# A two-layer conditioned transformer on one core: first scale and first projections by feature chunks, loads in that order

## The reference

```python
def ada_rms(x, t, w, tw):
    n = x * rsqrt(mean(square(x), -1) + 1e-6)
    scale = t @ tw.T
    return n * (w * (1.0 + scale))[:, None, :]

h = ada_rms(x, time_emb, ln1_w, ln1_tw)
q, k, v = h @ Wq.T, h @ Wk.T, h @ Wv.T          # 8 query heads, 1 key/value head of 64
q, k = rope(q, pos), rope(k, pos)
x = x + softmax(q k^T / 8) v @ Wo.T
h = ada_rms(x, time_emb, ln2_w, ln2_tw)
x = x + (silu(h @ Wg.T) * (h @ Wu.T)) @ Wd.T    # inner width 2048
# then the second layer: layer norm with scale and shift from the condition (W_ada), attention with rope, add
```

## Time and profile before

| | us |
|---|---|
| median of 3 runs (lowest to highest) | 836.48 (835.95 to 837.05) |
| profiled execution | 836.44 |
| its span, first to last instruction | 834.6 |
| TensorE busy in the span | 827.2 |
| VectorE, ScalarE, GpSimd busy | 598.5, 414.1, 392.4 |

### The profile page before, as it was taken

The page is one execution under the profiler, slowest core; times in us unless marked ns, Lnnn a source line. Parts: engine busy times, 40 slices in busy tenths (PEclk is TensorE's granted clock), DMA queues, the critical chain, the costliest instruction groups (busy, mean ns, idle before and its releaser), DMA issues.

```text
span 834.6 us, 15041 instructions
## 1 busy us (share of the span) xinstructions
PE 827.2 (99%) x5688; PEld 678.6 (81%) x5688; DVE 598.5 (72%) x889; ACT 414.1 (50%) x725; POOL 392.4 (47%) x310
## 2 busy tenths in 40 slices
PE   9999999999999999999999999999999999999998
PEld 5888878888788788787888887888878878878886
DVE  6986567666665766766656878877867668678997
ACT  4555445435345344345446475373453543735662
POOL 2667535545544446446545755454443533532110
PEclk9999999999999999999999999999999999999999
DMA  9913442433523523424444445355254353330001
GB/s 334 387 34 110 137 158 98 162 119 116 175 101 104 183 92 131 158 68 154 145 154 143 144 166 196 115 177 169 83 184 155 105 196 124 124 132 14 15 27 52
DMA packets 73335, 113.50 MB, mean 136 GB/s; under 512 B 6320, under 2 KB 39088, under 8 KB 73264
## 3 DMA queue, kind: packets, MB, share of 16 engines
q1 hardware_dynamic: 72544, 112.45, 39.8%
q10 hardware_dynamic: 720, 0.09, 0.1%
HBM read 88.15 MB, written 24.38 MB: 135 GB/s over the span
## 4 chain that ended last, share of the span: by engine, by line
PE 95%; DVE 2%; DMA 1%; issue 1%; ACT 0%; POOL 0%; SPq 0%; ACTq 0%; DVEq 0%; POOLq 0%
PE ps L736 29%; PE ps L738 28%; PE ps L737 28%; PE ps L1024 2%; PE ps L834 1%; PE ps L1052 1%; PE ps L783 1%; DMA pT<-turned_p 1%; PE ps L864 1%; PE ps L775 1%; DVE ex L1529 1%; PE ps L1032 1%; PE ps L745 1%; PE ps L992 0%; DMA turned_p<-tp 0%
## 5 line engine op out<-in xcount | busy, mean ns | idle before, releaser
L736 PE MATMUL ps<-h2h,guh 128*128 128x512 f32 x512 | 203.5, 397 | 0.0
L738 PE MATMUL ps<-h2l,guh 128*128 128x512 f32 x512 | 199.9, 391 | 0.0
L737 PE MATMUL ps<-h2h,gul 128*128 128x512 f32 x512 | 199.3, 389 | 0.0
L590 POOL TENSOR_TENSOR gul<-rgu,guh 128x1024 fp32r<-128x1024 f32 x64 | 161.0, 2516 | 71.2 <-ACT guh L1890 71.2
L595 POOL TENSOR_TENSOR wdl<-rwd,wdh 128x512 fp32r<-128x512 f32 x64 | 83.5, 1304 | 129.4 <-ACT wdh L1898 129.4
L1415 DVE TENSOR_TENSOR xres<-ps,xres 128x512 f32<-128x512 f32 x128 | 87.4, 684 | 62.7 <-PE ps L738 62.7
L736 PEld LDWEIGHTS ps<-h2h,guh 128*128 128x128 f32 x512 | 96.0, 188 | 27.4 <-issue 7.7
L738 PEld LDWEIGHTS ps<-h2l,guh 128*128 128x128 f32 x512 | 96.1, 188 | 21.2
L737 PEld LDWEIGHTS ps<-h2h,gul 128*128 128x128 f32 x512 | 96.2, 188 | 19.1
L736 PE MATMUL ps<-wdh,ah 128*128 128x512 f32 x256 | 100.1, 391 | 0.0
L737 PE MATMUL ps<-wdh,al 128*128 128x512 f32 x256 | 99.6, 389 | 0.0
(11 more groups left out here) (199 smaller groups left out, 1588.1 us busy)
## 6 DMA issues: line engine op xcount, KB each, us to landing
rgu<-gu SPq DMA_DIRECT2D x64, 512.0 KB, 4.7
rwd<-WdT SPq DMA_DIRECT2D x64, 256.0 KB, 4.2
turned_q<-tq SPq DMA_DIRECT2D x20, 320.0 KB, 3.0
qkT<-turned_q SPq DMA_DIRECT2D x20, 320.0 KB, 3.2
turned_p<-tp SPq DMA_DIRECT2D x9, 512.0 KB, 2.6
pT<-turned_p SPq DMA_DIRECT2D x9, 512.0 KB, 4.0
xt<-xT SPq DMA_DIRECT2D x15, 256.0 KB, 2.9
out<-xres SPq DMA_DIRECT2D x15, 256.0 KB, 3.5
```

Source lines behind the costliest of these rows:

```text
L590: pool.tensor_tensor(gul[i][:, :], rgu[i][:, :], guh[i][:, :], ALU.subtract).then_inc(m_gul, 1)
L736: pe.matmul(dst, lh, rh, start=start, stop=False)
L737: pe.matmul(dst, ll, rh, start=False, stop=False)
L738: return pe.matmul(dst, lh, rl, start=False, stop=stop)
```

## The change

The first scale is no longer computed for all 512 features at once. `first_scale(g)` computes 128 of them, g = 0 to 3, with four products that add up in one strip of 32 columns (strip g); ScalarE copies those 32 rows, `first_scale_T(g)` transposes them to 128x32, VectorE makes the scale of chunk g of them, and chunk g of the turned `x` is scaled by VectorE for tile 0 (`scale_part`, one 128x128 multiply) and by ScalarE for tile 1 (two activations of 128x64). `first_qkv(t, k)` is now two products, of one chunk, and the chunks of both tiles alternate with the scale groups. Half of `condition_second` moves ahead of `qk_T(0)`. `ln1_tw` is laid out by output group; SyncE loads group, `WqkvT` chunk, group, chunk and so on, with `xT` of tiles 0 and 1 after the first group and chunk. The five small loads on ScalarE's queue become two, one for the positions and one (`consts`) that holds the identity, the norm weights and the rope frequencies. The loads of `ln2_tw`, `adaT` and `x` of tiles 3 to 5 are cut into parts with semaphores of their own. `square(2)`, `mean_sq(2)`, `low_h(2)`, `split_qkv` and `scale_h(2)` take other places in the lists of their engines. The last `keep_warm(3)` stays; the three single ones become one. The results are the same sums.

The core of the diff (semaphore counts and declarations left out):

```diff
@@ SyncE @@
-            sp.dma_start(condt[:, :, :], by_row(condT)).then_inc(ld_cond, 16)
-            for k in range(KT):
-                sp.dma_start(adaw0[:, k, :], by_row(ln1_twT)[:, k, :]).then_inc(ld_ln1[k], 16)
-            load_xT(0)
-            for k in range(KT):
-                sp.dma_start(wst[:, k, :], by_row(WqkvT)[:, k, :]).then_inc(ld_qkv[k], 16)
-            sp.dma_start(xres[:, 0, :], xv[:, 0, :]).then_inc(ld_x0, 16)
-            load_xT(1)
+            sp.dma_start(condt[:, :, :], condT).then_inc(ld_cond, 16)
+            for g in range(KT):
+                sp.dma_start(adaw0[:, g, :], ln1_tw[g, :, :]).then_inc(ld_ln1[g], 16)
+                if g == 0:
+                    load_xT(0)
+                if g == KT - 1:
+                    sp.dma_start(xres[:, 0, :], xv[:, 0, :]).then_inc(ld_x0, 16)
+                sp.dma_start(wst[:, g, :], by_row(WqkvT)[:, g, :]).then_inc(ld_qkv[g], 16)
+                if g == 0:
+                    load_xT(1)
             sp.dma_start(xres[:, 1, :], xv[:, 1, :]).then_inc(ld_x1, 16)
-            sp.dma_start(adaw1[:, :, :], by_row(ln2_twT)).then_inc(ld_ln2, 16)
+            for k in range(KT):
+                sp.dma_start(adaw1[:, k, :], by_row(ln2_twT)[:, k, :]).then_inc(ld_ln2[k], 16)
-            sp.dma_start(adaw2[:, :, :], by_row(adaT)).then_inc(ld_ada, 16)
+            for i, ks in enumerate((slice(0, 1), slice(1, KT))):
+                sp.dma_start(adaw2[:, ks, :], by_row(adaT)[:, ks, :]).then_inc(ld_ada[i], 16)
+            sp.dma_start(xres[:, 3, :], xv[:, 3, :]).then_inc(ld_x3, 16)
             load_xT(3)
-            sp.dma_start(xres[:, 3:6, :], xv[:, 3:6, :]).then_inc(ld_x3, 16)
+            sp.dma_start(xres[:, 4:6, :], xv[:, 4:6, :]).then_inc(ld_x4, 16)
             sp.dma_start(rope1t[:, :, :], rope1).then_inc(ld_rope1, 16)
@@ GpSimd @@
             rstd(1)
+            rope_sum(0)
             low_h(2)
-            rope_sum(0)
+            rope_sum(1)
             rstd(2)
@@ TensorE @@
+            def first_scale(g):
+                pe.wait_ge(ld_ln1[g], 16)
+                rows = slice(NB * g, NB * (g + 1))
+                for k in range(KT):
+                    mm = pe.matmul(ps[rows, first_bank(g), 0:P], condt[:, k, :], adaw0[:, g, P * k:P * (k + 1)],
+                                   start=(k == 0), stop=(k == KT - 1), tile_position=(0, NB * g))
+                mm.then_inc(first_mm, 1)
+
+            def first_scale_T(g):
+                pe.wait_ge(first_sb, g + 1)
+                rows = slice(NB * g, NB * (g + 1))
+                pe.transpose(ps[:, first_bank(g), P:P + NB], tq[rows, 0:P], idn[rows, rows],
+                             tile_position=(NB * g, 0)).then_inc(first_T, 1)
-            def first_qkv(t):
-
-                pe.wait_ge(a_hf, t + 1)
-                for k in range(KT):
-                    pe.wait_ge(ld_qkv[k], 16)
-                    for c in range(2):
-                        mm = pe.matmul(ps[:, qkv_banks(t)[c], 0:QK0], xt[t][:, k, :],
-                                       wst[:, k, QK0 * c:QK0 * (c + 1)],
-                                       start=(k == 0), stop=(k == KT - 1))
-                mm.then_inc(a_qkv, 1)
+            def first_qkv(t, k, between=None):
+
+                pe.wait_ge(a_xs[t], k + 1)
+                pe.wait_ge(ld_qkv[k], 16)
+                for c in range(2):
+                    mm = pe.matmul(ps[:, qkv_banks(t)[c], 0:QK0], xt[t][:, k, :],
+                                   wst[:, k, QK0 * c:QK0 * (c + 1)],
+                                   start=(k == 0), stop=(k == KT - 1))
+                    if c == 0 and between is not None:
+                        between()
+                if k == KT - 1:
+                    mm.then_inc(a_qkv, 1)
             keep_warm(4)
             pe.wait_ge(ld_cond, 16)
-            for k in range(KT):
-                pe.wait_ge(ld_ln1[k], 16)
-                mm = condition(k, in_blocks(adaw0, k))
-                if k < KT - 1:
-                    keep_warm(1)
-            mm.then_inc(ada_mm, 1)
-            pe.wait_ge(ld_idn, 16)
-            condition_T(1, 1, BD[0])
+            first_scale(0)
+            keep_warm(1)
+            pe.wait_ge(ld_const, 16)
+            first_scale_T(0)
             keep_warm(3)
-            first_qkv(0)
-            first_qkv(1)
+            first_qkv(0, 0)
+            first_scale(1)
+            first_qkv(1, 0, lambda: first_scale_T(1))
+            first_scale(2)
+            first_qkv(0, 1)
+            first_scale_T(2)
+            first_scale(3)
+            first_qkv(1, 1)
+            first_scale_T(3)
+            first_qkv(0, 2)
+            first_qkv(0, 3)
+            first_qkv(1, 2)
+            first_qkv(1, 3)
+            condition_second((0, 1))
             qk_T(0)
-            condition_second()
+            condition_second((2, 3))
             scores(0)
-            condition_T(2, 1, BG)
+            condition_T(1, 1, BG)
             qkv(2, lambda: qk_T(1))
             p_T(0)
             condition_last((0,))
@@ VectorE @@
+            def first_scale(g):
+                dve.wait_ge(first_T, g + 1)
+                dve.scalar_tensor_tensor(out=sc_ln1[:, g, :], in0=ps[:, first_bank(g), P:P + NB], scalar=1.0,
+                                         in1=lnw[:, 0, g:g + 1].broadcast_to([P, NB]),
+                                         op0=ALU.add, op1=ALU.mult).then_inc(first_done, 1)
+
+            def scale_part(k):
+                dve.wait_ge(first_done, k + 1)
+                if k == 0:
+                    dve.wait_ge(ld_xt[0], 16)
+                h = xt[0][:, k, :].rearrange("p (b s) -> p b s", b=2)
+                dve.tensor_tensor(h, h, sc_ln1[:, k, 0:2].unsqueeze(2).broadcast_to([P, 2, S]),
+                                  ALU.mult).then_inc(a_xs[0], 1)
+
             dve.tensor_scalar(turns, angle, 1.0 / TWO_PI, ROUND, ALU.mult, ALU.add).then_inc(ang_step, 1)
+            first_scale(0)
+            scale_part(0)
+                if part == C2:
+                    first_scale(1)
+                    scale_part(1)
-            adaptive_scale(0, sc_ln1, BD[0])
-            scale_h(0)
-            angles_end()
+            first_scale(2)
+            scale_part(2)
             split_qkv(0)
+            first_scale(3)
+            scale_part(3)
+            mean_sq(0)
             split_qkv(1)
-            mean_sq(0)
-            scale_h(1)
+            scale_h(2)
+            mean_sq(1)
+            rope_mul(0)
             split_qkv(2)
-            mean_sq(1)
-            scale_h(2)
-            rope_mul(0)
             split_qkv(3)
-            mean_sq(2)
             keys(0)
             rope_mul(1, lambda: softmax_sub(0))
+            mean_sq(2)
             softmax_norm(0)
@@ ScalarE @@
-            act.dma_start(invt[:, :], invf).then_inc(ld_pos, 16)
-            act.dma_start(idn[:, :], ident).then_inc(ld_idn, 16)
-            act.dma_start(lnw[:, 0, :], ln1_w).then_inc(ld_lnw, 16)
-            act.dma_start(lnw[:, 1, :], ln2_w).then_inc(ld_lnw, 16)
+            act.dma_start(consts[:, :], small).then_inc(ld_const, 16)
+            def first_scale_copy(g):
+                act.wait_ge(first_mm, g + 1)
+                rows = slice(NB * g, NB * (g + 1))
+                act.copy(tq[rows, 0:P], ps[rows, first_bank(g), 0:P]).then_inc(first_sb, 1)
+
+            def scale_part(k):
+                act.wait_ge(first_done, k + 1)
+                if k == 0:
+                    act.wait_ge(ld_xt[1], 16)
+                for b in range(2):
+                    h = xt[1][:, k, S * b:S * (b + 1)]
+                    ins = act.activation(h, h, ACT.Copy, scale=sc_ln1[:, k, 2 + b:3 + b])
+                ins.then_inc(a_xs[1], 1)
             act.activation(spare[:, :], minus_half[:, :], ACT.Sin)
-            condition_copy(1, 1)
+            first_scale_copy(0)
             split_qkv(0)
+            scale_part(0)
+            first_scale_copy(1)
+            split_qkv(1)
+            scale_part(1)
+            first_scale_copy(2)
+            split_qkv(2)
             rope_table(0)
-            split_qkv(1)
+            first_scale_copy(3)
+            scale_part(2)
             rope_table(1)
             square(0)
-            split_qkv(2)
+            scale_part(3)
             split_qkv(3)
             square(1)
             high_h(2)
-            square(2)
             values(0)
             act.activation(spare_exp[:, :], minus_half[:, :], ACT.Exp)
             queries(0)
-            condition_copy(2, 1)
+            condition_copy(1, 1)
+            square(2)
             high_wo(0)
             values(1)
             softmax_exp(0)
```

More of the change, by code:

```diff
@@ L46, in fill, with build @@
         next(pieces, None)
-def build(nc, x, xT, pos, condT, ln1_w, ln1_twT, ln2_w, ln2_twT, WqkvT, WoT, gu, WdT,
-          adaT, b_ada, Wq1T, Wkd, wkvuT, Wo1T, invf, rope1, ident, out):
+def build(nc, x, xT, pos, condT, ln1_tw, ln2_twT, WqkvT, WoT, gu, WdT,
```

(11 more changed lines are left out.)

86 lines of the change are left out of this document (48 added, 38 removed).

## The result

The changed kernel takes 841.49 us (median of 5 runs, 841.06 to 842.36) where the kernel before took 836.48 beside it: a ratio of 1.0063, with a 95% interval of 1.0051 to 1.0074. The forecast was 841.0 within 836.6 to 843.0. The profiled execution took 841.06 us, its span is 839.2.

A forecast was written before the change was run, and what follows sets the result against it. The prediction took TensorE's own queue to bound the kernel: 836.44 - 2.05 (earlier start) + 2.5 (scale groups) + 0.3 (transposes) + 1.9 (shape changes) + 1.9 (waits and covers lost up to `qk_T(1)`) = 841.0 us, range 836.6 to 843.0.

The forecast's parts named there:

- Loads: Loads at the start: reordering, extra issues on SyncE and merging ScalarE's small loads change nothing, 0 us.
- Start of the projections: First projection product on TensorE: starts at 9.1 us instead of 11.17, a gain of 2.05 us.
- 1.7 us at the slow pace, to 6.5: First scale group on TensorE: four products in one strip from 4.81 us, 0.42 each at 1.2 GHz.
- If the start comes before 8: Sign of being wrong: the first projection product starting before 8 us, where 9.1 was forecast.
- The projections: TensorE's 16 products: 8.85 us plus groups 2.5, small transposes 0.3 and shape changes 1.9, ending at 22.65 instead of 20.02.
- strips beside the full products: Rival: strip products and small transposes between projections cost TensorE no time of their own; 835.1 us, chance 0.07.
- changes of shape are free: Rival: the 1.9 us of shape changes between projections vanish and ScalarE's and VectorE's chains bound; 838.1 us, chance 0.13.
- `qk_T(0)`: Tile 0 on TensorE: comes at 23.8 us, waiting for `rope_sum(0)` 0.4 us after TensorE is ready.
- Scores: Tile 0's scores on TensorE: wait for `keys(0)` behind two splits, at 25.5 us instead of 21.72, 3.8 late.
- I take 1.8 for both, between 1.6 and 2.7: The two VectorE splits ahead of `keys(0)`: 1.8 us together, one of them beside `low_h(2)`.
- `qk_T(1)`: Tile 1 on TensorE: 3.54 us after `keys(0)` starts, at 28.85 us instead of 24.36, 4.5 late.
- A constant distance afterwards.: After `qk_T(1)` both kernels do the same in the same order, so the lateness stays constant.

The follow-up runs named there:

- a2: The changed kernel run again, unaltered, beside the kernel before on one chip: 842.56 us, ratio 1.0076.
- f1: e3 with the fourth split also ahead of `mean_sq(1)` on VectorE and its cast ahead of tile 1's rope table on ScalarE: 841.16 us, ratio 1.0062.
- e2: The changed kernel with the four products of scale groups 1 to 3 each done twice, same result: 845.61 us, ratio 1.0117.
- e1: The changed kernel with every first-scale product and small transpose at the full tile shape, so no shape changes between projections: 840.34 us, ratio 1.0056.
- g1: e3 with `square(2)`, `mean_sq(2)` and `rstd(2)` moved earlier, so `low_wo(0)` follows `rope_sum(1)` at once: 839.31 us, ratio 1.0035.
- l1: The kernel before with only identity, norm weights and rope frequencies merged into one tile and one load: 837.00 us, ratio 1.0010.
- c1: The changed kernel with the first scale computed whole, side by side in four strips, ahead of the projections: 839.41 us, ratio 1.0038.
- d3: c1 with queues in order of need, all splits ahead of `mean_sq(1)`, and small tiles and loads as before: 836.33 us, ratio 0.9999.
- e4: The changed kernel with GpSimd's `low_wo(0)` held back until tile 0's probabilities are ready: 842.01 us, ratio 1.0076.
- e3: The changed kernel with VectorE's splits each one place earlier, so only one stands ahead of `keys(0)`: 840.20 us, ratio 1.0053.

## Why the prediction was right, and where its steps were not

The total was right to 0.1 us in the profiled execution, and the reason given holds: TensorE carries 4.3 us more in the stretch of the projections, and VectorE's queue comes late on top. But the terms were off by some 2 us in each direction, and cancelled: up to `qk_T(0)` the kernel is 1.8 us earlier than forecast, and behind it 1.9 us more are lost than the sum had. That the total was met so closely is luck; by the ratio of a2 the loss is 6.4 us where 4.6 were forecast. The low end of the prediction's own sum, 839.8, doesn't follow from its terms either: with 0.14 us for a change of shape and 1.6 for the splits they give about 840.4.

**Loads.** Worth nothing, as said: TensorE's order of time shows no wait for a load in the start of the changed kernel.

**Start of the projections.** Forecast 9.1, measured 7.65. The step "1.7 us at the slow pace, to 6.5" failed: the four products began 0.3 us earlier, at 4.48, took 1.0 us, and the `zeros` behind them ran fast as well. "If the start comes before 8" was one of the prediction's signs of being wrong, and it came true. In a2 the start was 8.54, in f1 8.88. I took the pace of one execution for a property of the kernel; the forecast lies beyond the slow end of what was seen.

**The projections.** Forecast 13.55 us, measured 13.19 in both profiles of the changed kernel. A product in a strip costs 0.22 (e2; forecast 0.21), a change of shape at least 0.13 (e1; forecast 0.17, up to 0.5 us too much in all). This was the largest term, and its mechanism is shown: "strips beside the full products" falls with e2, "changes of shape are free" with e1.

**`qk_T(0)`.** Forecast 23.8, measured 21.96; both follow the end of the projections by 1.1 us, and the wait for `rope_sum(0)` was 0.48 where 0.4 stood. The whole difference is that of the two terms above.

**Scores.** The order was read rightly, `keys(0)` behind two splits. The term "I take 1.8 for both, between 1.6 and 2.7" was mis-sized: they took 3.10. I let one of them run beside GpSimd; both did. The first takes 1.36, and the second, from 22.5 to 24.4, 1.89. I had also misread the 1.36 of the earlier trace rows: `low_h(2)` was over at 18.59 there, and the split at 19.28 stood beside the second sum of `rope_sum(0)`, as the first does here:

```profile
19.23 0.73 POOL L575 TENSOR_TENSOR qr<-t 128x256 f32<-128x256 f32 x1
```

No row of the kernel before shows a split beside `low_h(2)`. The Trainium skill's page "SBUF — State Buffer", section "SBUF: two separate sides", says that a VectorE instruction with two inputs in SBUF and a GpSimd instruction that reads SBUF exclude each other: the one that starts first holds the shared ports for its whole length. The rows agree: `rope_sum(0)` ends at 21.91 and the first split 0.68 later; `low_h(2)` ends at 23.71 and the second split 0.68 later; `low_wo(0)` ends at 30.10 and the multiply of the softmax 0.55 later. So VectorE's instruction pays all that is left of GpSimd's, and `low_h(2)`, issued during the first split, paid 0.57 in its turn. The two key parts before the splits took 0.4 us less than the 1.2 that I had taken from the earlier trace rows.

**`qk_T(1)`.** Forecast 4.5 us late, measured 3.5. It followed the copy of the keys by 3.52 us, as in the kernel before; the rest is the copy's date.

**"A constant distance afterwards."** This step failed. `p_T(0)` adds 0.6 us, because `rstd(2)`, which I set to 0, pushes `low_wo(0)` beside the last multiply of the softmax. What "falls into a wait of its engine" still moves what stands behind it; g1 takes this back. Another 0.5 us come later, in the second layer, where l1 shows that the merged small tile alone costs some 0.6. I had set it to 0 as a matter of loads.

**Where the loss came from.** Of 6.35 us (a2 and the kernel before in one batch), the scale between the projections is 3.15 (c1), the merged tile some 0.6 (l1), and the places in the queues the other 2.6 (d3, by difference). For the full change g1 recovers 2.3 us of 5.3 by the ratios. In its profile the rest is 2.0 us at `qk_T(0)` (projections 3.5 us earlier, 4.3 longer, then 1.1 of second scale and wait) and 0.8 in the second layer. No variant is faster than the kernel before by more than the measurement tells; the best, d3, is equal to it.

What stays open: why the pace doubles at another moment in another execution of one kernel, how much of the difference between the changed kernel's two medians that makes, what took e4's gain, and what grows by 0.12 us a tile in l1. Three of the changed kernel's five executions also show a mean granted clock of 0.998, as e4's profiled one does, and none of a2's; where it fell in them was not recorded.

## What to carry to other kernels

Where a kernel is bound by TensorE, work that stands side by side in strips is cheap only there: cut into groups and placed between full products, each product costs its whole 0.22 us and each change of shape 0.13, however early it lets the next stage begin. When work changes places in one engine's list, walk the lists of the others and ask what now stands ahead of the instruction that the bound engine waits for next; here one subtraction too many ahead of a copy of 0.28 us was worth 1.4 us (e3), about half of the 2.6 us that no work explains. And an instruction moved into a gap is free only if what stands behind it doesn't move into another engine's way.

## What the runs showed of the hardware

- VectorE and GpSimd stretch each other where both read SBUF: a split of 0.82 us took up to 1.89 beside `low_h(2)`, which took 1.85 instead of 1.28, and a multiply of 0.69 took 1.60. It shows as a longer instruction and not as idle time.
- TensorE's pace at the start doubles at different moments in different executions: the first group after the `zeros` took 1.03 us in the changed kernel's profile, 1.60 in a2's, 1.92 in f1's, with the same instructions. It moves the start of the projections by 1.2 us. The profile's granted clock reads 1.00 throughout.
- The granted clock fell to 0.61 and 0.58 in stretches of four microseconds after TensorE had waited (e4, c2), and not in other profiles with the same wait of 1.69 us in the weight loads (the changed kernel, a2, c1).
- Merging a few small tiles and their loads made the tiles of the second layer some 0.12 us longer between 485 and 719 us (l1), by what is not known.
